# Layer 1's shift in four 32-row tiles over pairs of PSUM units, and first score units in 64x64 tiles

## What is computed

```python
tq, sq = _expmap0_split(q)
tk, sk = _expmap0_split(k)
neg_inner = jnp.einsum('bhie,bhje->bhij', tq, tk) - jnp.einsum('bhid,bhjd->bhij', sq, sk)
dist = jnp.arccosh(jnp.maximum(neg_inner, 1.0 + 1e-07))
scores = -dist ** 2 / np.sqrt(D)
scores = jnp.where(causal[None, None], scores, -jnp.inf)
attn = jax.nn.softmax(scores, axis=-1) * spike_mask
y = jnp.einsum('bhij,bhjd->bhid', attn, v)
```

## Time and profile before

| | |
|---|---|
| median of 3 runs | 1960.74 us (1958.33 to 1961.65) |
| profiled execution | 1960.27 us, its span 1958.5 us |
| busy | PE 92%, ACT 86%, DVE 84%, POOL 55% of the span |
| mean granted TensorE clock | 0.983 of full speed |

### The profile page before, as it was taken

One profiled execution on the slowest core, in us unless ns is written; L12 is line 12 of the kernel. 1 busy time (PEld: TensorE's weight loads), 2 busy tenths in 40 slices (PEclk: granted clock), 3 DMA queues, 4 the chain that ended last, 5 costly groups with the idle time before them and its releaser, 6 DMA issues.

```text
span 1958.5 us, 51866 instructions
## 1 busy us (share of the span) xinstructions
PE 1792.7 (92%) x17922; PEld 1354.0 (69%) x17922; DVE 1646.1 (84%) x3472; ACT 1679.3 (86%) x2270; POOL 1079.7 (55%) x1208
## 2 busy tenths in 40 slices
PE   4668999999999999999999999999999999999987
PEld 2446777777777777777777777777777777777676
DVE  7788888888888888888888888888888888988884
ACT  8437988889898888989888898988889898887898
POOL 5336655556655555665555666555566655556533
PEclk9778999999999999999999999999999999999999
DMA  7332233233223322323332232333233233323110
GB/s 212 101 90 66 72 90 93 70 70 92 67 70 89 91 70 70 92 64 74 89 91 70 71 90 62 77 89 91 66 75 87 61 81 89 91 62 77 48 47 7
DMA packets 302073, 154.98 MB, mean 79 GB/s; under 512 B 14372, under 2 KB 298052, under 8 KB 302020
## 3 DMA queue, kind: packets, MB, share of 16 engines
q1 hardware_dynamic: 302020, 154.29, 31.4%
HBM read 82.41 MB, written 71.30 MB: 78 GB/s over the span
## 4 chain that ended last, share of the span: by engine, by line
issue 37%; POOL 26%; PE 22%; ACT 7%; DVE 5%; SPq 1%; POOLq 1%; DMA 0%; DVEq 0%; ACTq 0%
POOL zs L1405 11%; PE pu L2260 5%; PE pav L2114 3%; POOL prob L1392 3%; POOL prob L1398 3%; POOL xn L1330 2%; ACT zs L1692 2%; POOL prob L1394 2%; ACT zc L1693 2%; PE pav L2117 1%; PE pm L2235 1%; POOL rs L1313 1%; PE pm L2222 1%; POOL rs L1320 1%; PE pu L2091 1%
## 5 line engine op out<-in xcount | busy, mean ns | idle before, releaser
L1405 POOL TENSOR_TENSOR zs<-zc,zs 128x1024 f32<-128x1024 f32 x192 | 452.3, 2364 | 141.0 <-ACT zc L1693 141.0
L2260 PE MATMUL pu<-hid,h1t 128*128 128x256 f32 x1024 | 252.3, 390 | 0.4 <-DVE nmax L771 0.4
L2260 PE MATMUL pu<-hid,h2t 128*128 128x256 f32 x1024 | 238.5, 381 | 0.0
L1383 POOL TENSOR_TENSOR emb<-xn,w_sur 128x256 f32<-128x256 f32 x32 | 23.5, 733 | 358.2 <-PE pm L2134 358.2
L1692 ACT ACTIVATE zs<-zc,mhalf 128x1024 f32<-128x1024 f32 x192 | 218.7, 1139 | 0.4
L1693 ACT ACTIVATE zc<-zc,phalf 128x1024 f32<-128x1024 f32 x192 | 218.1, 1136 | 0.0
L2260 PEld LDWEIGHTS pu<-hid,h1t 128*128 128x128 f32 x1024 | 185.4, 191 | 40.9 <-issue 20.3
L758 DVE TENSOR_REDUCE zmin<-pu 128x4 f32<-128x1024 f32 (+1 forms) x154 | 187.7, 1219 | 23.9 <-DVE hid L976 16.9
L2260 PEld LDWEIGHTS pu<-hid,h2t 128*128 128x128 f32 x1024 | 187.1, 190 | 22.3 <-issue 0.5
L1713 ACT ACTIVATE zs<-zs 128x1024 f32<-128x1024 f32 x192 | 197.2, 1046 | 2.1 <-POOL zs L1405 2.1
L955 DVE TENSOR_SCALAR zc<-pu 128x1024 f32<-128x1024 f32 x154 | 186.7, 1212 | 0.0
(11 more groups left out here) (316 smaller groups left out, 4752.5 us busy)
## 6 DMA issues: line engine op xcount, KB each, us to landing
scr<-parts SPq DMA_DIRECT2D x256, 192.0 KB, 2.4
q_st<-scr SPq DMA_DIRECT2D x128, 256.0 KB, 3.9
scr<-parts SPq DMA_DIRECT2D x128, 128.0 KB, 2.4
k_st<-scr SPq DMA_DIRECT2D x64, 256.0 KB
k_st<-scr SPq DMA_DIRECT2D x32, 512.0 KB, 5.1
x<-in_L_attn_x SPq DMA_DIRECT2D x32, 128.0 KB, 3.3
out<-xold SPq DMA_DIRECT2D x32, 128.0 KB, 1.8
q_st<-m_t SPq DMA_DIRECT2D x128, 4.0 KB
```

Source lines behind the costliest of these rows:

```text
L1405: G.tensor_tensor(zs[:, c], zc[:, c], zs[:, c], ALU.add).then_inc(sum_done.sem, 1)
L2260: last = PE.matmul(u.ap[:, c * T:(c + 1) * T], w[:, k, c * P:(c + 1) * P], src[:, k, :], start=(k == 0), stop=(k == HC - 1))
```

## The change

- `sel` and `m_t[1]` now hold the shift four times, once in each strip of 32 rows (16 rows of the rounded part, 16 of the remainder). For that, ACT's `minima_log` writes a bf16 copy of the squares into `nmax_parts` beside `nmax[1]`, DVE's `minima_lo` writes the remainder there (in place of `shift_lo`, at an earlier place), and PE's `minima_t` (in place of `maxima_t`) transposes both by eight matmuls of 128x32 tiles; ACT's `shift_part` copies all 128 rows and frees the buffer.
- `squares_by_key` becomes `squares_t` (the transposes) and `squares_shift` (the shift, each matmul in a tile of 32 rows by 128 columns, each of four strips on a bank of its own). In the loop body the shift follows the second unit of a pair: (0, 1), (2, 3), (4, 5). In the closing it follows each unit.
- sub1 moves from AV to U0, after min4.
- `first_scores` splits each 64x128 matmul by query into two of 64x64.

```diff
-        U0_USES = ... + uses(L, ["min3", "min4"]) + uses(E, ["sub3", "sub5"]) + uses(L, ["min5"]) + ...
+        U0_USES = ... + uses(L, ["min3", "min4"]) + uses(E, ["sub1", "sub3", "sub5"]) + uses(L, ["min5"]) + ...
-        AV_USES = ... + uses(M, ["exp3", "av0"]) + uses(E, ["sub0", "sub1"]) + uses(F, ["max0"]) + ...
+        AV_USES = ... + uses(M, ["exp3", "av0"]) + uses(E, ["sub0"]) + uses(F, ["max0"]) + ...
...
+            def minima_lo(e):
+                dve.wait_ge(squares_ready.sem, squares_ready.at(e))
+                V.tensor_tensor(nmax_parts[:, :, 1, :], nmax[1][:], nmax_parts[:, :, 0, :], ALU.subtract).then_inc(lo_ready.sem, 1)
...
                     clamp_cosh(run, 2)
+                if e:
+                    minima_lo(e)
                 if m:
                     attended(run, m, 0)
                     attended(run, m, 1)
-                if e:
-                    shift_lo(run, "mT1", 1, e)
...
-                S.activation(nmax[1][:].rearrange("p k h -> p (k h)"), zd[:], ACT.Square).then_inc(squares_ready.sem, 1)
+                S.activation(nmax[1][:].rearrange("p k h -> p (k h)"), zd[:], ACT.Square)
+                S.activation(nmax_parts[:, :, 0, :], zd[:].rearrange("p (k h) -> p k h", k=BLK), ACT.Square).then_inc(squares_ready.sem, 1)
...
                 u.wait_free(pe)
+                apart(pe)
                 for s in range(4):
                     for e in range(2):
-                        PE.matmul(u.ap[:, o:o + P], q_st[layer][halves[e], pair, e, 0:P], k, start=(s == 0), stop=False)
+                        for a in range(2):
+                            PE.matmul(u.ap[halves[a], o:o + P], q_st[layer][halves[e], pair, e, a * QW:(a + 1) * QW], k, start=(s == 0), stop=False)
...
+            def squares_shift(run, ns):
+                if ns[0] == 0:
+                    misc(run, "mT1").wait_drained(pe)
+                first = ns[0] < 2
+                for s in range(4 if first else 2):
+                    for strip, (n, b) in enumerate((n, b) for n in ns for b in range(2)):
+                        u, r = unit(run, f"sub{n}"), slice(32 * strip, 32 * strip + 32)
...
+                        done = s == (3 if first else 1)
+                        last = PE.matmul(out, sel[r, h, :], shift, start=False, stop=done)
+                        if done and b == 1:
+                            last.then_inc(u.full, 1)
...
+            def minima_t(run, e):
+                pe.wait_ge(lo_ready.sem, lo_ready.at(e))
+                u.wait_free(pe)
+                for k in range(BLK):
+                    for strip in range(0, P, 32):
+                        last = PE.matmul(u.ap[strip:strip + 32, k * P:(k + 1) * P], nmax_parts[:, k].rearrange("p n h -> p (n h)"), ident_bf[:], start=True, stop=True)
...
                 if e:
-                    squares_by_key(run, unit(run, "sub1"), e, 1)
+                    squares_t(run, e, 1)
+                    squares_shift(run, (0, 1))
                 if m:
                     project1(run, 1, "qkv1b")
                     project1(run, 0, "qkv1a")
                 if e:
-                    squares_by_key(run, unit(run, "sub2"), e, 2)
-                    squares_by_key(run, unit(run, "sub3"), e, 3)
-                    squares_by_key(run, unit(run, "sub4"), e, 4)
+                    squares_t(run, e, 2)
+                    squares_t(run, e, 3)
+                    squares_shift(run, (2, 3))
+                    squares_t(run, e, 4)
                 if f:
                     project_latent(run, f)
                 if e:
-                    squares_by_key(run, unit(run, "sub5"), e, 5)
+                    squares_t(run, e, 5)
+                    squares_shift(run, (4, 5))
```

More of the change, by code:

```diff
@@ L1148, in closing @@
                 remote_bias(r0)
+                minima_lo(r0.end)
                 attended(r0, r0.middle, 0)
@@ L1208, in closing @@
                 latent_norm(r1, k1[M])
+                minima_lo(r1.end)
                 attended(r1, r1.middle, 0)
-                shift_lo(r1, "mT1", 1, r1.end)
                 attended(r1, r1.middle, 1)
@@ L1239, in closing @@
                 spikes(r2.end, k2[E])
-                shift_lo(r2, "mT1", 1, r2.end)
+                minima_lo(r2.end)
                 output(r2, r2.out)
@@ L1265, in closing @@
                 attention_out(r2, r2.end)
-                shift_lo(r3, "mT1", 1, r3.end)
+                minima_lo(r3.end)
                 square_log(r3.end, 0)
@@ L2496, in closing @@
                 window_scores(unit(r0, "max3"), 3)
-                squares_by_key(r0, unit(r0, "sub4"), r0.end, 4)
-                squares_by_key(r0, unit(r0, "sub5"), r0.end, 5)
+                squares_t(r0, r0.end, 4)
+                squares_shift(r0, (4,))
+                squares_t(r0, r0.end, 5)
+                squares_shift(r0, (5,))
                 feed(unit(r0, "f2"), h1t, hid1, 2)
@@ L2542, in closing @@
                 scores_by_key(unit(r1, "exp3"), 3)
[L2543 to L2544 removed]
+                minima_t(r1, r1.end)
                 attend(avuse(r1, "av0"), 0, 0, r1.middle)
@@ L2563, in closing @@
                 project1(r1, 0, "qkv1a")
-                squares_by_key(r1, unit(r1, "sub4"), r1.end, 4)
-                squares_by_key(r1, unit(r1, "sub5"), r1.end, 5)
+                squares_t(r1, r1.end, 4)
+                squares_shift(r1, (4,))
+                squares_t(r1, r1.end, 5)
+                squares_shift(r1, (5,))
                 feed(unit(r1, "f2"), h1t, hid1, 2)
@@ L2594, in closing @@
                 feed(unit(r2, "f3"), h2t, hid2, 3)
-                squares_by_key(r2, unit(r2, "sub0"), r2.end, 0)
-                squares_by_key(r2, unit(r2, "sub1"), r2.end, 1)
-                squares_by_key(r2, unit(r2, "sub2"), r2.end, 2)
-                squares_by_key(r2, unit(r2, "sub3"), r2.end, 3)
-                squares_by_key(r2, unit(r2, "sub4"), r2.end, 4)
-                squares_by_key(r2, unit(r2, "sub5"), r2.end, 5)
+                squares_t(r2, r2.end, 0)
+                squares_shift(r2, (0,))
+                squares_t(r2, r2.end, 1)
+                squares_shift(r2, (1,))
+                squares_t(r2, r2.end, 2)
+                squares_shift(r2, (2,))
+                squares_t(r2, r2.end, 3)
+                squares_shift(r2, (3,))
+                squares_t(r2, r2.end, 4)
+                squares_shift(r2, (4,))
+                squares_t(r2, r2.end, 5)
+                squares_shift(r2, (5,))
                 second_scores(unit(r2, "min2"), 2)
@@ L2623, in closing @@
                 feed(unit(r3, "f3"), h2t, hid2, 2)
[L2624 to L2625 removed]
+                minima_t(r3, r3.end)
                 feed(unit(r3, "f3"), h2t, hid2, 3)
[L2627 to L2632 removed]
+                squares_t(r3, r3.end, 0)
+                squares_shift(r3, (0,))
+                squares_t(r3, r3.end, 1)
+                squares_shift(r3, (1,))
+                squares_t(r3, r3.end, 2)
+                squares_shift(r3, (2,))
+                squares_t(r3, r3.end, 3)
+                squares_shift(r3, (3,))
+                squares_t(r3, r3.end, 4)
+                squares_shift(r3, (4,))
+                squares_t(r3, r3.end, 5)
+                squares_shift(r3, (5,))
                 pe.wait_ge(vst_ready.sem, vst_ready.at(r3.end))
```

121 lines of the change are left out of this document (57 added, 64 removed).

## The result

The changed kernel takes 2209.56 us, the median of four runs (2208.34 to 2210.64), against 1961.07 (1958.33 to 1961.65) for the kernel before on the same chip: a ratio of 1.1262, 95% interval [1.1248, 1.1275]. The forecast was 2208. The profiled execution took 2209.07 us, its span is 2207.3 us and the mean granted clock of its TensorE 0.931.

The account below looks back on a forecast made before the run. A ring of waits through PE, ACT and POOL was taken to bound each round. 28 rounds x (6.25 stalls + 2.5 clock) = 245, plus 3 for the closing, on 1960.3 gave 2208 us; range 2125 to 2245.

Parts of the forecast that it names:

- The ring, and what bounds the kernel: Each round: 24.4 us from attend av0 to embT on PE, then 32.8 through ACT and POOL to the next attend.
- sub1 waits for min4's clamp: In each loop round, PE stands 3.1 us ahead of sub1 until DVE's clamp of min4 frees U0.
- ACT waits for sub0: ACT's weights1(0) waits for the pair's shift and holds x1T's copy; project1 starts 5.0 us later, embT 6.25 a round.
- The signs that were named: Profile after: about 66 us rounds; idle about 3 before sub1, 6 before weights1, over 2 before project1; PE busy time down.
- the case that the clock holds: Rival: the clock stays up through the loop's stall, so 28 x 6.25 + 3 = 178 us, 2138 us; chance 0.17.
- The clock: PE's granted clock falls to 1.2 GHz once every loop round after the stall, costing 2.5 us (0 to 3.6).
- PE's work falls by 2.0 us: Per round on PE: cheaper shift, first scores and minima_t, less added shape changes, save about 2.0 us.
- Four tiles side by side: On PE, four 32-row shift matmuls run together, so the shift costs a quarter: 0.22 us a pair, 0.66 a round.
- rival 4: The shift's tiles don't go side by side on PE: +56 us on the forecast, 2264 us; chance 0.05.
- The closing: In the second closing round minima_t waits for minima_lo ahead of attend, +2.3 us; +3 (0 to 6) taken overall.

Follow-up runs that it names:

- filler: The kernel after with seven unused 128x384 matmuls a loop round added in PE's two stalls, so that PE stays busy: 2159.89 us.
- noshift: The kernel before with the shift's matmuls left out of the loop body, so the shift is not subtracted there: 1948.44 us.
- sub1_av: The kernel after with the loop's shifts of units 0 and 1 each following their own unit, and sub1 back in AV: 1993.78 us.
- split01: The kernel after with the loop's shifts of units 0 and 1 each following their own unit; sub1 stays in U0 behind min4: 2137.09 us.
- act_order: The kernel after with ACT's weights1(0) moved behind its copies of f3 and x1T: 2140.81 us.
- minima: The kernel before with only the new minima path (ACT's second square, minima_lo, minima_t, 128-row copy); shift in full-array matmuls unit by unit, old buffers: 1971.14 us.
- closing: The kernel after with DVE's minima_lo moved earlier in the second and third closing rounds, loop untouched: 2201.32 us.

## Why the prediction was right, point by point

Filler is the kernel after at full clock, and so the one that the prediction's steps can be set against. All times in us from the start of attend av0; "predicted" from the dates in the text, less 1044.26. The rows are those shown above, with three more of filler's ACT timeline and two of its DVE timeline:

```profile
1223.72 1.02 ACT L1741 ACTIVATE prob<-pav 128x1024 f32<-128x1024 f32 x1 [6.10 <-PE pav L2122]
...
1225.55 0.39 ACT L1635 ACTIVATE xn_t<-pm 128x256 f32<-128x256 f32 x1
...
1230.34 1.94 ACT L1741 ACTIVATE prob<-pu 128x1024 f32<-128x1024 f32 x2 [1.51 <-PE pu L2122]
```

```profile
1220.99 1.22 DVE L962 TENSOR_SCALAR zc<-pu 128x1024 f32<-128x1024 f32 x1
...
1235.14 0.23 DVE L943 TENSOR_SCALAR emb<-ctime 128x64 f32<-128x64 f32 x1
```

```
step                          predicted   filler   after (clock falls)
U0 free, clamp of min4 done     16.9      16.96    16.95
ACT weights1(0)                 18.3      18.47    19.38
project1                        20.6      20.74    21.65
ACT weights1(2)                 24.9      25.09    28.17
DVE embedding done              30.0      30.12    33.21
embT                            30.6      30.94    34.03
```

- *The ring, and what bounds the kernel.* Right. From embT to the next attend it is 1301.51 - 1268.65 = 32.9 us in the kernel after, and was 32.8. noshift shows the other side: PE was the busiest engine and 2.7 us less of its work are worth 0.45 a round.
- *sub1 waits for min4's clamp, ACT waits for sub0.* Right, and shown: sub1_av and split01 take them away, act_order the second alone. They were priced at 6.25 us a round and cost 6.55 (filler). The largest miss among the steps is 0.3. The signs that were named are there, as 2.74, 7.01 and 2.31 us of waiting ahead of sub1, `weights1(0)` and `project1`, but for one: PE's busy time was to go down, and rose. (For the case that the clock holds, 57.25 + 6.25 makes rounds of 63.5, not 63.4.)
- *The clock.* The mechanism was right: it falls in every round, within 1.7 us behind the end of the first stall. The size was set too high: 2.5 taken, 1.9 measured. Two things speak against one price per fall. The lower level costs unequally: 7.8 us of it a round cost 1.9 in the kernel after, and in act_order some rounds with 3.4 us of it are no longer than those with none (62.5 to 62.6), since the slower work takes the place of a wait for ACT, as the two rounds shown there have it. And its length changes with the idle stretches of a round, as act_order (3.8 us a round) and split01 (5.3) show.
- *PE's work falls by 2.0 us.* Too much, as far as busy time tells. From 200 to 1780 us the kernel before has PE busy 1508.36 of 1580 us and sub1_av 1453.32, both at a clock of 1.00: 54.65 and 53.33 us a round, 1.3 less. Filler without its added matmuls has 1.1 less. Busy time reads low here, though: noshift, with 2.7 us of shift gone by the starts of the rows, has 2.2 less of it. It changes nothing, because PE doesn't set the end.
- *Four tiles side by side.* Right, so rival 4 falls. In filler the pair's shift lies between 1223.28 and 1223.62: sixteen matmuls in 0.34 us, which is four rounds of 0.056 and 0.1 for the changes of shape, as priced. The 32-row tile is no slower than the 64-row one.
- *The closing.* This is the term that was mis-sized: +3 (0 to 6) taken. To the end the kernel after has 22.0 us more, of which the last round is 8.5: 13.5 for the closing, and 12.9 of them come with the minima's path alone (minima). The delay of the second closing round was foreseen, at 2.3 us from attend's old start. It is 3.7 (in the wait of 5.3 is also the 1.3 that PE stood for POOL there before), because `minima_lo`, taken at 0.2 us, lasts 1.9. Behind it attend runs at the lower clock, which costs 2.4 more: the prediction put a price on a fall of the clock in the loop and none in the closing. In the third round a smaller wait was allowed for, and it is 1.7, though `minima_lo` itself takes only 0.2 there; the one of 3.8 in the fourth was not counted (the kernel before stands 1.3 us for ACT there). These two rounds add 6.8.

The errors had opposite signs. Stalls and closing were 8 us (28 x 0.3) and 10 us too low, the clock 17 us too high (28 x 0.6). Besides, the kernel after reached the marker of round 3 1.9 us earlier (172.24 against 174.11); in the twelve kernels it lies between 170.8 and 175.1, so this is not put down to the change. That the sum is off by 2 us is partly luck. The clock's term lies within its bounds (0 to 3.6), the closing's does not.

## What to carry to other kernels

Before PE work is made cheaper, find which wait ends the round and what the work is worth there. Here removing the shift altogether was worth 13 us, while moving a unit to a buffer that comes free later, and sharing one completion between two units, cost 216. An in-order engine turns a late unit into a late everything: ACT's `weights1(0)` held two copies that had long been ready, and one line's move gave back 69 us. A gap that opens in PE once a round should be priced with the clock. Ask of a fall not what the stall costs but which of the slower instructions end the round.

## What the runs showed of the hardware

**A small VectorE operation that lasts as long as GpSimd's.** `minima_lo` subtracts two SBUF tensors of 128x32. Its 32 executions take 194 ns at the least and 2322 at the most. DVE's timeline in the round shown and in the fourth closing round, and POOL's beside them:

```profile
1236.11 1.15 DVE L830 TENSOR_TENSOR nmax_parts<-nmax,nmax_parts 128x32 bf16<-128x32 f32 x1
...
2179.14 2.32 DVE L830 TENSOR_TENSOR nmax_parts<-nmax,nmax_parts 128x32 bf16<-128x32 f32 x1 [6.06 <-ACT nmax_parts L1716]
```

```profile
1236.04 1.18 POOL L1352 TENSOR_TENSOR resid<-qk_t,parts 128x512 f32<-128x512 f32 x1
...
2176.77 4.64 POOL L1412 TENSOR_TENSOR zs<-zc,zs 128x1024 f32<-128x1024 f32 x2
```

Each ends with an instruction of POOL: 1236.11 + 1.15 = 1237.26 and 1236.04 + 1.18 = 1237.22; 2181.46 and 2181.41. It is so in 31 of the 32, to within 53 ns, always with a TENSOR_TENSOR of POOL; the one with no POOL instruction beside it is the one of 194 ns. In one (251.72 us) it was kept through the end of one POOL instruction and through the two that followed. In the run closing, the same operation, moved to where POOL stands idle, takes 0.18 us (at 2086.96) instead of 1.88. The Trainium skill (SBUF — State Buffer, SBUF: two separate sides) says that VectorE and GpSimd share a pair of ports by an exclusive lock, that a VectorE operation with two SBUF inputs needs it against a GpSimd operation that reads SBUF, and that the loser is blocked for the whole instruction of the other. This trace agrees, and shows one thing more at 251.72: VectorE can stay blocked through several instructions of GpSimd in a row. In the profile the blocked time counts as busy, so no view of waits names it: min and max of one tile do. In the loop it hides behind attend (rounds of 57.20 in minima). In the closing the second and the fourth round pay for it (1.88 and 2.32 us); in the third, `minima_lo` takes its 0.19 and comes late for another reason, its place in DVE's order.

**The clock.** In the kernel after the granted clock falls in every round from round 4 on, for 6.8 or 10.2 us at 0.50. This bears out the rule that the prediction drew on (the Trainium skill, TensorE: Matmul & The Clock Gate, HAM oscillation: a PE idle for long enough in each pass is throttled in each pass). In act_order, with the 2.7 us stall alone left, two of 27 rounds have none.
